# Block 1's attention probabilities: 32x32 blocks turned by VectorE and placed through a scratch in memory, in place of TensorE transposes and ScalarE copies

## What is computed

```
q = _rope(_heads(xq @ wq)); k = _rope(_heads(ctx @ wk)); v = _heads(ctx @ wv)
sim = jnp.einsum('bhnd,bhmd->bhnm', q, k) * DH ** (-0.5)
a = jax.nn.softmax(sim, axis=-1)
o = jnp.einsum('bhnm,bhmd->bhnd', a, v)
x = o.transpose(0, 2, 1, 3).reshape(...) @ wo + bo + x
```

## Time and profile before

| | |
|---|---|
| median of 3 runs | 4207.89 us (4205.87 to 4213.07) |
| span of the profiled execution | 4201.7 us |
| TensorE busy | 4066.9 us, 97% |
| VectorE, ScalarE, GpSimd busy | 2877.2, 2728.2, 2864.3 us (68%, 65%, 68%) |
| parts 3 and 4 (block 1's attention) | from about 1560 to 3830 us |
| mean DMA traffic | 66 GB/s |

### The profile page before, as it was taken

One profiled execution on the slowest core, in us unless ns is written; L12 is line 12 of the kernel. 1 busy time (PEld: TensorE's weight loads), 2 busy tenths in 40 slices (PEclk: granted clock), 3 DMA queues, 4 the chain that ended last, 5 costly groups with the idle time before them and its releaser, 6 DMA issues.

```text
span 4201.7 us, 95690 instructions
## 1 busy us (share of the span) xinstructions
PE 4066.9 (97%) x34870; PEld 3481.4 (83%) x34870; DVE 2877.2 (68%) x6098; ACT 2728.2 (65%) x10756; POOL 2864.3 (68%) x2674
## 2 busy tenths in 40 slices
PE   7999999999999999999999999999999999999999
PEld 6777777777789988888888888888888888888998
DVE  7888889999865556565656565777676767664443
ACT  6999998888943336666666666666666666665333
POOL 5777777777767776565666666666666666666776
PEclk9999999999999999999999999999999999999999
DMA  2101111111111122212121212322222222221110
GB/s 83 32 32 32 32 44 42 42 47 47 58 46 51 56 73 74 79 67 84 69 81 71 81 71 95 105 85 84 86 84 86 81 87 80 89 99 55 41 51 31
DMA packets 230899, 276.63 MB, mean 66 GB/s; under 512 B 38044, under 2 KB 160416, under 8 KB 230432
## 3 DMA queue, kind: packets, MB, share of 16 engines
q1 hardware_dynamic: 230364, 270.51, 19.0%
q10 hardware_dynamic: 68, 0.02, 0.0%
HBM read 85.89 MB, written 50.33 MB: 32 GB/s over the span
## 4 chain that ended last, share of the span: by engine, by line
PE 80%; ACT 8%; DVE 6%; issue 3%; POOL 3%; DMA 0%; ACTq 0%; SPq 0%; DVEq 0%; POOLq 0%
PE BANKS L616 18%; PE BANKS L617 16%; PE BANKS L618 16%; PE BANKS L810 7%; PE BANKS L774 7%; PE BANKS L762 6%; ACT PR L913 5%; PE BANKS L696 3%; PE BANKS L832 2%; DVE WL L1101 1%; PE BANKS L743 1%; ACT HF L960 1%; ACT WH L897 1%; DVE PT L1064 1%; PE BANKS L629 1%
## 5 line engine op out<-in xcount | busy, mean ns | idle before, releaser
L1248 POOL TENSOR_TENSOR PR<-PR,RL 128x512 f32<-128x512 f32 x1024 | 1068.1, 1046 | 686.1 <-DVE RL L1069 685.6
L929 ACT ACTIVATE PR<-BANKS,NM 128x128 f32<-128x128 f32 x2048 | 729.0, 382 | 444.0 <-DVE NM L1115 437.7
L913 ACT ACTIVATE PR<-BANKS,NM 128x128 f32<-128x128 f32 x2048 | 728.6, 414 | 12.7 <-DVE NM L1056 10.5
L616 PE MATMUL BANKS<-HH,WH 128*128 128x512 f32 x1632 | 689.8, 423 | 2.4 <-ACT HF L960 1.6
L810 PE MATMUL BANKS<-ID,PR 128*128 128x128 f32 x4096 | 623.7, 275 | 58.5 <-DVE OL L1108 24.0
L1115 DVE TENSOR_REDUCE NM<-BANKS 128x8 f32<-128x1024 f32 x256 | 313.4, 1224 | 487.7 <-PE BANKS L774 487.7
L617 PE MATMUL BANKS<-HL,WH 128*128 128x512 f32 x1632 | 643.4, 394 | 0.0
L618 PE MATMUL BANKS<-HH,WL 128*128 128x512 f32 x1632 | 641.4, 393 | 0.0
L810 PEld LDWEIGHTS BANKS<-ID,PR 128*128 128x128 f32 x4096 | 488.6, 140 | 181.9 <-POOL PR L1248 54.5
L913 ACT ACTIVATION_READ_ACCUMULATOR PR<-BANKS,NM 128x1 f32 x2048 | 521.4, 255 | 0.0
L929 ACT ACTIVATION_READ_ACCUMULATOR PR<-BANKS,NM 128x1 f32 x2048 | 452.5, 221 | 0.0
(11 more groups left out here) (133 smaller groups left out, 10701.1 us busy)
## 6 DMA issues: line engine op xcount, KB each, us to landing
SW<-SN SPq DMA_DIRECT2D x1024, 128.0 KB, 2.0
x_scratch<-X SPq DMA_DIRECT2D x80, 512.0 KB, 3.2
X<-x_scratch SPq DMA_DIRECT2D x80, 512.0 KB, 4.0
CX<-in_ctx SPq DMA_DIRECT2D x32, 384.0 KB, 4.0
X<-in_x SPq DMA_DIRECT2D x16, 512.0 KB, 3.8
out<-X SPq DMA_DIRECT2D x16, 512.0 KB, 2.9
CX<-in_ctx SPq DMA_DIRECT2D x32, 128.0 KB, 4.3
STG<-in_L_xcond_W SPq DMA_DIRECT2D x4, 512.0 KB, 5.3
```

The lines of the kernel that those rows point to most:

```text
L616: e.matmul(o, lh, rh, start=first and i == 0, stop=False)
L913: made = e.activation(pr[:, r], bank[:, r], ACT.Exp, bias=nm[:, h:h + 1], accum_out=RL[npr(t)[0]][:, h:h + 1])
L929: made = e.activation(pr[:, r], bank[:, r], ACT.Exp, bias=nm[:, h:h + 1], accum_out=RL[npr(t)[0]][:, h:h + 1])
L1248: e.tensor_tensor(p3, p3, RL[npr(t)[0]][:, :].unsqueeze(2).broadcast_to([128, 4, 128]), ALU.mult).then_inc(s_nrm, 1)
```

## The change

In parts 3 and 4 `p_turn` and `p_copy` go, and three stages take their place:

- `blocks`, two ticks after a tile's exponentials: VectorE transposes the 32x32 blocks of the 128x512 tile, each block in its place of partitions, and writes them in an order in which the key block `j` comes first (TR, two buffers of 128x1024, one buffer for both tiles of a unit).
- `put`, tau+4: SyncE writes TR to a scratch in memory (`p_scratch`, four slots of 512 KB) with one DMA.
- `get`, tau+5: SyncE waits until that has landed and reads it back with four DMAs of 128 KB. Each fills 32 partitions of PB (three buffers) from all four query blocks, in runs of 1 KB.

`pv` moves from tau+6 to tau+8, `low` with it, and `out` from tau+7 to tau+9; `v1` moves from tau-1 to tau+1. Some weight pieces of part 4 are split two ticks later. `pv` reads its moving operand as four runs of 32 columns, 256 elements apart. Transposed probabilities no longer use a bank, so the three banks serve `v1`, `q1`, `k1` and the input transposes. ScalarE's exponentials now wait for VectorE's blocks of the tile four earlier. A reservation in SBUF that GpSimd's DMAs would use is made smaller, and no such DMA exists here.

```diff
-NP1, NPT1 = 4, 4
+NP1, NTR, NPT1, NSC = 4, 2, 3, 4
...
-                    for stage, lag in (("q1", -5), ("q1_add", -3), ("k1", -4), ("k1_add", -2), ("scores", 0), ("max", 0), ("pv", 6), ("low", 6),
-                                       ("out", 7)):
+                    for stage, lag in (("q1", -5), ("q1_add", -3), ("k1", -4), ("k1_add", -2), ("scores", 0), ("max", 0), ("put", 4), ("get", 5),
+                                       ("pv", 8), ("low", 8), ("out", 9)):
...
-                    at["v1", tick - 1].append((p, g, j))
+                    at["v1", tick + 1].append((p, g, j))
...
-                        for stage, lag in (("exp", 0), ("normal", 1), ("p_turn", 3), ("p_copy", 3)):
+                        for stage, lag in (("exp", 0), ("normal", 1), ("blocks", 2)):
...
+            TR = [sb(f"TR{i}", [128, 1024], stack=spare) for i in range(NTR)]
...
+        PB = [sb(f"PB{i}", [128, 4, 256]) for i in range(NPT1)]
...
+        PSC = nc.dram_tensor("p_scratch", [NSC, T, 1024], F, kind="Internal").ap()
...
+                for x in at["put", tick]:
+                    q.wait_ge(s_tr, 2 * x.i + 2)
+                    q.wait_ge(s_pv, x.i - NSC + 1)
+                    e.dma_start(PSC[x.i % NSC], TR[x.i % NTR][:, :]).then_inc(s_put[x.i % NTR], 16)
+                for x in at["get", tick]:
+                    q.wait_ge(s_put[x.i % NTR], 16 * (x.i // NTR + 1))
+                    q.wait_ge(s_pv, x.i - NPT1 + 1)
+                    turned = PSC[x.i % NSC].rearrange("(i c) (j k) -> j c i k", i=4, j=4)
+                    for j in range(4):
+                        e.dma_start(PB[x.i % NPT1][32 * j:32 * j + 32, :, :], turned[j]).then_inc(s_get[x.i % NPT1], 16)
...
-                    q.wait_ge(s_pt_a, NL0 // 4 + 2 * x.i + 2)
+                    q.wait_ge(s_get[x.i % NPT1], 64 * (x.i // NPT1 + 1))
...
-                            made = e.matmul(PS[5][64 * e_:64 * e_ + 64, 128 * b:128 * b + 128], V1[4 * (x.j // 4) + b][:, h:h + 64],
-                                            PT[(2 * x.i + e_) % NPT1][:, 128 * b:128 * b + 128], start=True, stop=True)
+                            k = 32 * (4 * e_ + b)
+                            made = e.matmul(PS[5][64 * e_:64 * e_ + 64, 128 * b:128 * b + 128].rearrange("p (i r) -> p i r", i=4),
+                                            V1[4 * (x.j // 4) + b][:, h:h + 64], PB[x.i % NPT1][:, :, k:k + 32], start=True, stop=True)
...
-                    q.wait_ge(s_t, max(NL0, t.n - NP1 + 1))
-                    q.wait_ge(s_nrm, max(NL0, t.n - NP1 + 1))
+                    q.wait_ge(s_t, NL0)
+                    q.wait_ge(s_tr, t.n - NL0 - NP1 + 1)
...
+                for t in at["blocks", tick]:
+                    i, e_ = divmod(t.n - NL0, 2)
+                    q.wait_ge(s_nrm, t.n + 1)
+                    q.wait_ge(s_pv0, NL0 // 4)
+                    q.wait_ge(s_put[i % NTR], 16 * (i // NTR))
+                    e.transpose(TR[i % NTR][:, :].rearrange("p (j k c) -> p j k c", j=4, k=8)[:, :, 4 * e_:4 * e_ + 4, :],
+                                PR[npr(t)[0]][:, :].rearrange("p (b j c) -> p j b c", b=4, j=4)).then_inc(s_tr, 1)
```

More of the change, by code:

```diff
@@ L231, in schedule @@
     chunks += [(e2 - 1, "sv", 0), (e2 - 1, "sv", 1), (e2 + 2, "so", 0), (e2 + 2, "so", 1)]
-    chunks += [(e3 - 13, "cq", 0), (e3 - 12, "ck", 0), (e3 - 8, "cv", 0), (e3 - 6, "cq", 1), (e3 - 5, "ck", 1), (e3 - 2, "cv", 1),
-               (e3 - 1, "co", 0), (e3 + 6, "co", 1)]
+    chunks += [(e3 - 13, "cq", 0), (e3 - 12, "ck", 0), (e3 - 6, "cv", 0), (e3 - 6, "cq", 1), (e3 - 5, "ck", 1), (e3, "cv", 1),
+               (e3 + 1, "co", 0), (e3 + 8, "co", 1)]
     chunks += [(e4 - 6, "f1", 0), (e4 - 5, "f1", 1), (e4 - 4, "f2", 0), (e4 - 3, "f2", 1)]
@@ L284, in build @@
             SW = [sb("SW0", [128, 512], stack=spare)]
-            sb("PT_L1", [128, 512 * NPT1], stack=spare)
+            TR = [sb(f"TR{i}", [128, 1024], stack=spare) for i in range(NTR)]
             SW += [sb("SW1", [128, 512], stack=spare)]
@@ L353, in build @@
         s_sw = [sem(f"sw{i}") for i in range(2)]
+        s_tr = sem("tr")
+        s_put = [sem(f"put{i}") for i in range(NTR)]
+        s_get = [sem(f"get{i}") for i in range(NPT1)]
         s_up, s_gf, s_gh, s_gl, s_dn = (sem(k) for k in ("up", "gf", "gh", "gl", "dn"))
@@ L374, in npt @@
         def npt(t):
-            k = t.n % NL0
-            return (k % NPT1, k - NPT1) if t.n >= NL0 else (k % NPT0, k - NPT0)
+            return t.n % NPT0, t.n - NPT0
         def pt_done(t):
-            if t.n >= NL0:
-                return s_pt_a, NL0 // 4 + t.n - NL0 + 1
             return (s_pt_a, t.n // 4 + 1) if t.u == 3 else (s_pt_d, 3 * (t.n // 4) + t.u + 1)
@@ L455, in build @@
             for t in at["p_turn", tick]:
-                tp.add(("p", t.n), FOUR if t.n < NL0 else THREE, *pt_done(t))
+                tp.add(("p", t.n), FOUR, *pt_done(t))
             for stage in ("turn", "c_turn"):
@@ L940, in _ @@
                 for t in at["p_copy", tick]:
-                    if t.n >= NL0 or t.u == 3:
+                    if t.u == 3:
                         q.wait_ge(s_t, t.n + 1)
[L943 to L948, removed]
+                        q.wait_ge(s_mod, 3)
+                        q.wait_ge(s_pv0, npt(t)[1] // 4 + 1)
                         e.activation(PT[npt(t)[0]][:, :], PS[tp.bank(("p", t.n))][:, :], ACT.Copy).then_inc(s_pt_a, 1)
@@ L1059, in _ @@
                 for t in at["p_copy", tick]:
-                    if t.n < NL0 and t.u != 3:
+                    if t.u != 3:
                         q.wait_ge(s_t, t.n + 1)
@@ L1333 @@
     from concourse.bass_utils import run_bass_kernel_spmd
-    nc = bacc.Bacc("TRN2", target_bir_lowering=False, num_devices=1)
+    nc = bacc.Bacc("TRN2", target_bir_lowering=False, num_devices=1, dynamic_dma_scratch_size=2048)
     arrays, aps = {}, {}
```

## The result

The changed kernel takes 4088.5 us (median of 4 runs, 4081.0 to 4091.7) beside 4207.7 us before: a ratio of 0.971, 95% interval 0.9698 to 0.9722. It is 119 us faster. The forecast was 4026 us, a gain of 182; the stated range of 3975 to 4170 holds the result, the forecast's own range of 3980 to 4060 does not.

What follows compares the result with a forecast made beforehand. TensorE's issue was taken to bound parts 3 and 4. The span: 4201.7 - 225 (transposes) + 38 (VectorE packing) + 5 (drain) = 4020 us, plus 6.2 to the median, 4026. Stated range 3975 to 4170; the forecast's own 3980 to 4060.

Steps and rivals of the forecast that it cites:

- The removal: TensorE, parts 3 and 4: dropping the transposes saves 0.44 us of chain twice a unit, 225 us in all.
- VectorE's transposes: VectorE, parts 3 and 4: two block transposes a unit at 0.68 us each, giving 6.61 and 7.49 us a unit.
- bad packing: VectorE's queue in part 4, at 96%, will not pack perfectly: 0.3 us a unit, 38 us.
- the drain: Longer lags where part 4 drains into the feed-forward: 5 us.
- Rival (a): VectorE's transposes cost about 1.22 us each and VectorE becomes the bound: 4105 us; 4060 to 4190, chance 0.19.
- The estimate of 1.24 us: Upper estimate for one 128x512 VectorE transpose, four 128x128 widths; VectorE would need 7.73 and 8.61 us a unit.
- SyncE and the DMAs: SyncE's queue in parts 3 and 4: five more issues and the landing wait fit the period; nothing charged.
- L: Time for put to land, on SyncE's queue: 3.2 to 3.5 us; may be 4.1 before SyncE binds.
- the turn of SyncE's queue: One unit's pass through SyncE's in-order queue: L + 3.7 us, 6.9 to 7.2 us, within the period.
- wrong if: Listed failure signs, among them TensorE waiting for get, transposes over 0.9 us, or pv's group adding over 1.02 us.
- Rival (b): SyncE's turn binds because put lands late; slower than before from L = 5.0, about 4325 us at 5.5; chance 0.10.
- pv's four runs: TensorE's pv reads its moving operand as four runs: nothing charged.

Runs made afterwards that it cites:

- no_dma: The changed kernel without put and get; VectorE's block transposes stay and pv reads a constant PB: 4020.0 us, ratio 0.9554.
- floor: The kernel before, with block 1's transposes of the probabilities and ScalarE's copies of them left out and nothing in their place: 3996.1 us, ratio 0.9495.
- pv10: The changed kernel with pv and low at tau+10 and out at tau+11, two ticks later: 4097.3 us, ratio 0.9739.
- get6_pv10: The changed kernel with get at tau+6 instead of tau+5, pv and low at tau+10 and out at tau+11: 4069.1 us, ratio 0.9669.

## Why the prediction was right, and where it was not

**The removal**: 225 us in the sum, 212 measured on its own. The slot of 0.44 us in the chain was the right price; the durations would have given 8 x 0.27 = 2.2 us a unit, two and a half times too much. The missing 13 us fit waits in part 4 that TensorE's fullness had hidden; no run takes them away.

**VectorE's transposes**: taken at 0.68 us, measured 0.687. Charged with 38 us for bad packing and 5 for the drain, together 43; measured 24 (no_dma against floor). The drain alone agrees: the last scores start at 3684.4 us instead of 3811.5, which is 127 us earlier, while the span is 122.5 us shorter, so about 5 us were given back behind them. In part 4 VectorE's load came out at 845.6 / 121 = 6.99 us a unit, not 7.49. Rival (a) did not occur, though the measured time lies in the band that it had. The estimate of 1.24 us from the Trainium skill's 311 ns ("VectorE: DVE Perf Modes", The three transpose paths) was nearly twice the measured 0.687. The Trainium skill's advice to use TensorE for a 128x128 transpose (same page, Rules for kernel authors) was not the better choice here, where TensorE was full: without it the kernel is 119 us faster.

**SyncE and the DMAs**: this step failed, with 0 in the sum against 68 us measured. Most of the parts that I worked out were right: L was 3.4 us, the turn of SyncE's queue fits the period, the DMA share came to 0.67 (0.6 said). The Trainium skill's formula for a landing ("DMA: Bandwidth & Descriptors", Anatomy of one DMA) is given there for DMAs that GpSimd issues, so the agreement of its 3.2 us with SyncE's store was no test of it. And an issue does not always cost 0.55 to 0.59 us: the issues of `get` ran from 0.30 to 2.03 us, with a median of 0.43. What I left out is who else waits on this queue. I asked whether SyncE could keep up on average and whether `pv` had slack. SyncE kept up. `pv`'s slack of three ticks was used up in part: TensorE waited 55 us for `get`, a sign that the prediction had listed as "wrong if", though longer lags in pv10 won nothing back. I did not ask how late the swaps would be for VectorE, which has two buffers and no slack, with the maxima queued behind, and for GpSimd's additions. It is the question of what stands behind a new wait, and here it had to be asked of the swaps behind `get` on SyncE and then of the products behind the swaps on VectorE. Rival (b) named this queue, but priced it as a throughput limit at L = 5.0; it acts as lateness at L = 3.4. Which of the late waits, VectorE's or GpSimd's, carries how much of the 68 us is open.

**pv's four runs**: nothing, as said. The group of 16 adds 1.02 us in the chain, as before:

```profile
2218.60 1.02 PE BANKS L775 x16
2219.62 1.09 PE BANKS L787 x16
```

Together: 4207.7 - 212 + 24 + 68 = 4088. Against the sum that is 13 us less gained, 19 us less lost on VectorE and the lags, and 68 us lost where nothing was charged, 62 us in all. That the stated range of 3975 to 4170 holds the time is luck in part: its high end was there for dear transposes, which did not come, and it caught a loss with another cause. A unit took 8.20 and 8.26 us, not the 7.9 and 8.1 that were to show the forecast. Of the 68 us, 39 go when the bytes are halved. The other 29 are open: get6_pv10, with the swaps never behind the wait for `put`, wins 19 of the 68 in whole work, but it changes the lags too.

## What to carry to other kernels

When work leaves the full engine, price it by what it adds to the chain, and price what replaces it in every in-order queue it enters: ask of each instruction behind the new waits who holds only two buffers of its result. A DMA queue with a third of its capacity to spare cost 68 us here, by being late for somebody. A stage in such a ring is worth moving only together with its consumer: `get` one tick later cost 291 us, and with `pv` moved two ticks it gained 19.

## What the hardware showed that I had not expected

VectorE's 32x32 block transpose of 128x512 float32, read and written in four interleaved pieces, takes 672 to 716 ns, as much as a two-operand instruction of that size (681 ns on average). TensorE reads a moving operand of four runs of 128 bytes at the speed of a contiguous one (273 ns at the median in `pv` before and after, 16 in 1.02 us of chain both times). A store of 256 KB from 64 partitions landed no sooner than one of 512 KB from 128 (3.4 us both). With the `get`s issued from a second queue three kinds of transfer landed later (swaps 2.7 to 3.0 us, `put` 3.4 to 4.1, `get` 3.1 to 3.2), at the same DMA share of 0.68; whether the second queue itself or the other moment of the issues does it was not tested. The X stores and loads did not (3.3 and 4.2 us, then 3.1 and 4.0).
